# Four-stage residual kernel: expert layers 1 and 2 with both activation parts in one product of 512 columns

## The reference

```python
x = x + L0(x, mask, cond_256, ...)   # attention, 16 heads of 16, RMS norm, modulation
x = x + L1(x, cond_256, ...)         # mixture of 8 experts, the 2 best per token
x = x + L2(x, cond_256, cond_64, ...)# low-rank map, its matrix orthogonalised first
x = x + L3(x, cond_256, ...)         # quaternion rotation
```

```python
h1 = relu(einsum('bsh,ehm->bsem', x, W1) + b1)     # 256 -> 512
h2 = relu(einsum('bsem,emn->bsen', h1, W2) + b2)   # 512 -> 512
out_e = einsum('bsen,enh->bseh', h2, W3) + b3      # 512 -> 256
return einsum('bseh,bse->bsh', out_e, cw)          # cw: softmax weights of the two best experts, else 0
```

## Time and profile before

| | |
|---|---|
| median of 3 runs | 1185.68 us (1181.59 to 1188.18) |
| span of the profiled execution, first to last instruction | 1176.1 us |
| what the page gives of that execution beyond its span | nothing; the median lies 9.6 us above the span |
| TensorE (PE) busy | 1132.8 us, 96% of the span |
| VectorE (DVE) busy | 814.5 us, 69% |
| ScalarE (ACT) busy | 734.6 us, 62% |
| GpSimd (POOL) busy | 524.7 us, 45% |
| expert stage, first to last hidden product | about 628 to 1130 us |

### The profile page before, as it was taken

How to read it: one execution, slowest core, us unless ns; L and a number is a source line. 1 busy time by engine, 2 the same in 40 slices (tenths; PEclk the granted TensorE clock), 3 DMA queues, 4 the chain that set the end, 5 groups by cost and what they waited for, 6 DMA issues and landing times.

```text
span 1176.1 us, 23436 instructions
## 1 busy us (share of the span) xinstructions
PE 1132.8 (96%) x7525; PEld 770.1 (65%) x7582; DVE 814.5 (69%) x2327; ACT 734.6 (62%) x1628; POOL 524.7 (45%) x837
## 2 busy tenths in 40 slices
PE   8899999999999999998988999999999999999988
PEld 4333433434334343342426999999999999999968
DVE  5888888787897878978774444346555555677747
ACT  2466667666676766666566656756666565666645
POOL 8324145583764846747471565346223222222220
PEclk8999999999999999999999999999999999999999
DMA  8655637468275572662726596936665765723536
GB/s 219 205 179 185 211 108 227 132 199 247 86 232 187 171 233 87 219 207 97 279 102 223 160 309 217 360 72 175 175 189 157 224 209 153 248 47 67 164 90 215
DMA packets 101616, 213.65 MB, mean 182 GB/s; under 512 B 10917, under 2 KB 71341, under 8 KB 93046
## 3 DMA queue, kind: packets, MB, share of 16 engines
q1 hardware_dynamic: 86038, 192.42, 49.8%
q0 software_dynamic: 14304, 18.69, 8.7%
q10 hardware_dynamic: 1152, 1.05, 0.4%
HBM read 239.28 MB, written 74.29 MB: 267 GB/s over the span
## 4 chain that ended last, share of the span: by engine, by line
PE 43%; POOL 2%; DMA 2%; DVE 2%; issue 1%; ACT 1%; SPq 1%; POOLq 0%; ACTq 0%
PE bank L1080 37%; PE bank L1239 1%; PE bank L1095 1%; DMA x<-yout,rows 1%; PE bank L1109 1%; PE bank L1199 1%; POOL routed L1952 1%; PE bank L1181 1%; DMA routed<-xw,idx 1%; PE bank L1274 0%; PE bank L1219 0%; POOL run L840 0%; DMA w_parts<-in_W 0%; POOL gt L840 0%; DVE tb L840 0%
## 5 line engine op out<-in xcount | busy, mean ns | idle before, releaser
L1615 DVE CUSTOM_DVE_ANT_0 junk<-bank,mneg 128x512 bf16<-128x512 f32 x512 | 335.6, 683 | 92.1 <-PE bank L1151 91.3
L1347 ACT ACTIVATE pt<-bank 128x512 f32<-128x512 f32 x512 | 301.8, 595 | 150.1 <-PE bank L1166 102.7
L1962 POOL DMA_INDIRECT x<-yout,rows x78 | 123.2, 1579 | 287.3 <-ACT yout L1425 242.7
L1080 PE MATMUL bank<-hid,w 128*128 128x256 f32 x1872 | 243.5, 287 | 3.8 <-DVE hid L1763 3.8
L1080 PEld LDWEIGHTS bank<-hid,w 128*128 128x128 f32 x1872 | 230.1, 191 | 5.7 <-issue 4.3
L1763 DVE TENSOR_TENSOR hid<-full,hid 128x256 fp32r<-128x256 f32 x312 | 132.3, 427 | 142.3 <-ACT full L1420 140.9
L1415 ACT ACTIVATE hid<-bank,biases 128x256 fp32r<-128x256 f32 x312 | 149.3, 479 | 96.1 <-PE bank L1080 94.7
L1166 PE MATMUL bank<-mneg,identb 128*128 128x512 bf16 x391 | 148.7, 380 | 0.0
L1420 ACT ACTIVATE full<-bank,biases 128x256 f32<-128x256 f32 x312 | 148.4, 476 | 0.0
L1080 PE MATMUL bank<-rowsT,w 128*128 128x256 f32 x936 | 123.0, 285 | 1.2 <-issue 1.2
L1181 PE MATMUL bank<-pt,vaug 128*17 128x512 f32 x1024 | 123.2, 599 | 0.7
(11 more groups left out here) (183 smaller groups left out, 1463.8 us busy)
## 6 DMA issues: line engine op xcount, KB each, us to landing
w<-split_weights SPq DMA_DIRECT2D x80, 1024.0 KB
w<-split_weights SPq DMA_DIRECT2D x40, 2048.0 KB
split_weights<-w_parts SPq DMA_DIRECT2D x64, 512.0 KB, 3.8
w_parts<-in_W SPq DMA_DIRECT2D x64, 256.0 KB, 4.5
split_parts<-parts SPq DMA_DIRECT2D x28, 384.0 KB, 2.6
rows<-routed SPq DMA_DIRECT2D x39, 258.0 KB, 3.6
stacks<-split_parts SPq DMA_DIRECT2D x36, 256.0 KB, 5.2
qst<-split_parts SPq DMA_DIRECT2D x24, 256.0 KB, 5.0
```

Of the source, the lines that this page charges most:

```text
L1080: product = T.matmul(ps, w[p], x[q], start=(k == 0 and n == 0), stop=(k == len(weights) - 1 and n == 2))
L1347: A.activation(pt[n % len(pt)][:, :], bank[3 + n % 2][:, :], ACT.Exp, scale=float(D) ** -0.5).then_inc(exped.sem, 1)
L1615: V.tensor_tensor_reduce(junk[n % 2][:, :], bank[n % 3][:, :], mneg[:, 0, st, :], 1.0, FLOOR, ALU.add, ALU.max, rowmax[gi % 2][:, hh, st:s ...
L1962: G.indirect_dma_start(x2_dram, bass.IndirectOffsetOnAxis(ap=rows[j % NS][:, tt, E + 1:E + 2].bitcast(U32), axis=0), yout[j % NY][:, tt], ...
```

## The change

Layers 1 and 2 keep the high and low part of an activation next to each other in one buffer, 256 + 256 columns. `wide_products` multiplies the high weight by both in one product of 512 columns, into all 512 columns of the bank, and the low weight by the high part in one of 256 columns, into the left half. So a block takes two products in place of three, and the sum of the two halves of the bank is the result. Layer 3 keeps its three products; only its indices change.

The halves are added outside TensorE. For each hidden step ScalarE now reads the right half with the bias (Identity) into `full`; VectorE adds the left half to it (`hidden_sum`, which also frees the bank); ScalarE takes ReLU of that, rounded, as the high part (`rectified`); VectorE computes max(full, 0) minus the high part (`hidden_low`). The second instruction of each engine is put behind the first one of the next hidden step: `rectify_hidden` and `split_hidden` run after the next step's first instruction, at the start of `layer3`, and at the start of `layer2(0, 0)`. At the end TensorE issues 16 more products of 512 columns, behind the last one of the program: 12 over 48 rows, in turn on the lower and the upper half of the array's rows, and 4 over all rows. Nothing reads them.

```diff
--- before.py
+++ after.py
@@ -577,8 +577,7 @@
 
 
     def tile_buffers(i):
-        return ([sb(f"rowsT{i}_{n}", [P, KT, TW], F32R) for n in range(2)], [sb(f"hid1_{i}_{n}", [P, HT, TW], F32R) for n in range(2)],
-                [sb(f"hid2_{i}_{n}", [P, HT, TW], F32R) for n in range(2)])
+        return (sb(f"rowsT{i}", [P, KT, 2, TW], F32R), sb(f"hid1_{i}", [P, HT, 2, TW], F32R), sb(f"hid2_{i}", [P, HT, 2, TW], F32R))
...
     rows_high = signal("rows_high", of("turn"))
-    rectified = signal("rectified", [(n, *at) for s, *at in order for n in (1, 2) if s == f"layer{n}"])
+    hidden_at = [(n, *at) for s, *at in order for n in (1, 2) if s == f"layer{n}"]
+    hidden_rest = signal("hidden_rest", hidden_at)
+    rectified = signal("rectified", hidden_at)
...
-    hidden_low = signal("hidden_low", [(n, *at) for s, *at in order for n in (1, 2) if s == f"layer{n}"])
+    hidden_sum = signal("hidden_sum", hidden_at)
+    hidden_low = signal("hidden_low", hidden_at)
...
-        freed = summed.at(tuple(at)) if name == "last" else rectified.at((int(name[-1]), *at))
+        freed = summed.at(tuple(at)) if name == "last" else hidden_sum.at((int(name[-1]), *at))
...
                     product = T.matmul(ps, w[p], x[q], start=(k == 0 and n == 0), stop=(k == len(weights) - 1 and n == 2))
+            return product
+
+        def wide_products(ps, weights, factors):
+            for k, ((high_part, low_part), x) in enumerate(zip(weights, factors)):
+                last = k == len(weights) - 1
+                both = x.rearrange("p n t -> p (n t)")
+                if last:
+                    T.matmul(ps[:, 0:TW], low_part, x[:, 0], start=False, stop=False)
+                product = T.matmul(ps[:, :], high_part, both, start=(k == 0), stop=last)
+                if not last:
+                    T.matmul(ps[:, 0:TW], low_part, x[:, 0], start=False, stop=False)
             return product
...
-                products(ps[:, 0:TW], [weights_of(j, 0, k * M + m * P, k * M + (m + 1) * P) for k in range(KT)],
-                         [[x[:, k, :] for x in rowsT[j % 2]] for k in range(KT)]).then_inc(multiplied[0].sem, 1)
+                wide_products(ps, [weights_of(j, 0, k * M + m * P, k * M + (m + 1) * P) for k in range(KT)],
+                              [rowsT[j % 2][:, k] for k in range(KT)]).then_inc(multiplied[0].sem, 1)
...
                 pe.wait_ge(*hidden_low.at((1, j, HT - 1)))
-                products(ps[:, 0:TW], [weights_of(j, 1, k * M + m * P, k * M + (m + 1) * P) for k in range(HT)],
-                         [[x[:, k, :] for x in hid1[j % 2]] for k in range(HT)]).then_inc(multiplied[1].sem, 1)
+                wide_products(ps, [weights_of(j, 1, k * M + m * P, k * M + (m + 1) * P) for k in range(HT)],
+                              [hid1[j % 2][:, k] for k in range(HT)]).then_inc(multiplied[1].sem, 1)
...
-                products(ps[:, 0:E], [[x[:, k, tt * P:(tt + 1) * P] for x in hid2[j % 2]] for k in range(HT)],
+                products(ps[:, 0:E], [[hid2[j % 2][:, k, n, tt * P:(tt + 1) * P] for n in range(2)] for k in range(HT)],
...
                          [[a[b % 2][:, k * E:(k + 1) * E] for a in (ab_hi, ab_lo)] for k in range(KT)]).then_inc(finished.sem, 1)
             else:
                 side_stage(step)
+        pe.wait_ge(*finished.at((B - 1, ST - 1)))
+        for n in range(6):
+            for half in range(2):
+                lanes = x2T_hi[0][half * 64:half * 64 + 48, 0]
+                T.matmul(bank[4 + half][:, :], lanes[:, n % 4 * P:(n % 4 + 1) * P], lanes, start=True, stop=True)
+        for n in range(4):
+            T.matmul(bank[4 + n % 2][:, :], x2T_hi[0][:, 0, n * P:(n + 1) * P], x2T_hi[0][:, 0], start=True, stop=True)
...
+
+        unrectified = []
+
+        def rectify_hidden():
+
+            for n, j, m in unrectified:
+                if j >= 2:
+                    act.wait_ge(*last_product(n, j - 2))
+                act.wait_ge(*hidden_sum.at((n, j, m)))
+                A.activation((hid1, hid2)[n - 1][j % 2][:, m, 0], full[(hidden_sum.value[n, j, m] - 1) % len(full)][:, :],
+                             ACT.Relu).then_inc(rectified.sem, 1)
+            unrectified.clear()
...
-                A.activation(rowsT[j % 2][0][:, :, :].rearrange("p k t -> p (k t)"), ps[:, :], ACT.Copy).then_inc(rows_high.sem, 1)
+                A.activation(rowsT[j % 2][:, :, 0], ps[:, :].rearrange("p (k t) -> p k t", k=KT), ACT.Copy).then_inc(rows_high.sem, 1)
             elif name in ("layer1", "layer2"):
                 n = int(name[-1])
                 j, m = at
                 ps, _ = hidden_bank(step)
+                place = hidden_sum.value[n, j, m] - 1
+                column = (n - 1) * HT + m
+                if step == ("layer2", 0, 0):
+                    rectify_hidden()
                 act.wait_ge(*multiplied[n - 1].at((j, m)))
                 act.wait_ge(*biases_loaded(j))
-                if j >= 2:
-                    act.wait_ge(*last_product(n, j - 2))
-                column = (n - 1) * HT + m
-                A.activation((hid1, hid2)[n - 1][j % 2][0][:, m, :], ps[:, 0:TW], ACT.Relu,
-                             bias=biases[j % NS][:, column:column + 1])
-                place = rectified.value[n, j, m] - 1
                 if place >= len(full):
                     act.wait_ge(hidden_low.sem, place - len(full) + 1)
-                A.activation(full[place % len(full)][:, :], ps[:, 0:TW], ACT.Relu,
-                             bias=biases[j % NS][:, column:column + 1]).then_inc(rectified.sem, 1)
+                A.activation(full[place % len(full)][:, :], ps[:, TW:2 * TW], ACT.Identity,
+                             bias=biases[j % NS][:, column:column + 1]).then_inc(hidden_rest.sem, 1)
+                rectify_hidden()
+                unrectified.append((n, j, m))
             elif name == "layer3":
                 j, tt = at
+                rectify_hidden()
                 act.wait_ge(*y_biased.at((j, tt)))
                 A.activation(yout[j % NY][:, tt], yout[j % NY][:, tt], ACT.Copy,
...
+
+        unsplit = []
+
+        def split_hidden():
+
+            for n, j, m in unsplit:
+                hi, lo = ((hid1, hid2)[n - 1][j % 2][:, m, part] for part in range(2))
+                if j >= 2:
+                    dve.wait_ge(*last_product(n, j - 2))
+                dve.wait_ge(*rectified.at((n, j, m)))
+                V.scalar_tensor_tensor(lo, full[(hidden_sum.value[n, j, m] - 1) % len(full)][:, :], 0.0, hi.bitcast(F32),
+                                       ALU.max, ALU.subtract).then_inc(hidden_low.sem, 1)
+            unsplit.clear()
...
@@ -1749,20 +1795,23 @@
             elif name == "turn":
                 j, = at
                 ps, _ = misc_bank(step)
-                hi, lo = (rowsT[j % 2][n][:, :, :].rearrange("p k t -> p (k t)") for n in range(2))
+                hi, lo = (rowsT[j % 2][:, :, n] for n in range(2))
                 dve.wait_ge(*rows_high.at((j,)))
-                V.tensor_tensor(lo, ps[:, :], hi.bitcast(F32), ALU.subtract).then_inc(rows_split.sem, 1)
+                V.tensor_tensor(lo, ps[:, :].rearrange("p (k t) -> p k t", k=KT), hi.bitcast(F32), ALU.subtract).then_inc(rows_split.sem, 1)
             elif name in ("layer1", "layer2"):
                 n = int(name[-1])
                 j, m = at
-                hi, lo = (part[:, m, :] for part in (hid1, hid2)[n - 1][j % 2])
-                h = full[(rectified.value[n, j, m] - 1) % len(full)]
-                if j >= 2:
-                    dve.wait_ge(*last_product(n, j - 2))
-                dve.wait_ge(*rectified.at((n, j, m)))
-                V.tensor_tensor(lo, h[:, :], hi.bitcast(F32), ALU.subtract).then_inc(hidden_low.sem, 1)
+                ps, _ = hidden_bank(step)
+                place = hidden_sum.value[n, j, m] - 1
+                if step == ("layer2", 0, 0):
+                    split_hidden()
+                dve.wait_ge(*hidden_rest.at((n, j, m)))
+                V.tensor_tensor(full[place % len(full)][:, :], ps[:, 0:TW], full[place % len(full)][:, :], ALU.add).then_inc(hidden_sum.sem, 1)
+                split_hidden()
+                unsplit.append((n, j, m))
             elif name == "layer3":
                 j, tt = at
+                split_hidden()
                 dve.wait_ge(*multiplied[2].at((j, tt)))
```

## The result

The changed kernel takes 1194.39 us (median of 5 runs, 1193.78 to 1195.04) against 1185.68 us for the kernel before on the same chip: ratio 1.0076, 95% interval 1.0057 to 1.0095. It is slower, where 1172.4 us was forecast and 1161 to 1185 given as the range. On a second chip the ratio was 1.0106 (1.0087 to 1.0125).

A forecast was written before the change was run, and what follows sets the result against it. The prediction took the expert stage as bound by TensorE's product price, set by the weight load. Terms -19.2 + 2.5 + 1.4 + 1.0 + 0.6 + 0.4 = -13.3 us gave 1172.4 us, range 1161 to 1185.

The forecast's parts named there:

- The bound: Expert stage: bound by the price of a TensorE product in a row of them, 119.4 ns.
- the first term: Products of layers 1 and 2: 20.5 ns saved per block, 936 blocks, -19.2 us.
- the two bounds of the step: Wide product in layers 1 and 2: 218 ns as taken, or 239 ns if fp32r is priced by column, gaining nothing.
- own sign of being wrong: In the timeline: wide products starting 0.24 us apart; also PE waiting at layer 2 in every tile.
- the column sets the price: Rival for layers 1 and 2: products give 0 to 2.5 us, 5.9 us of waits stay, 1189 to 1191.5 us; chance 0.11.
- Tile 0: Start of layer2(0, 0): last layer 1 subtraction stands behind attention's last transpose on VectorE; +1.4 us (0 to 2).
- Routing steps: PE waits at 793.69 and near 700 us: ReLU and bank release now hang on VectorE too; +1.0 us (0 to 4).
- The building of the last matrices: Tiles beside it: VectorE side steps make the last subtraction about 0.8 us late in two tiles; +2.5 us (0 to 6).
- The elimination stretch: Tiles beside elimination steps: low parts ready with margins of 0.6 us, so no wait of PE on VectorE.
- The last tile: No layer 1 covers it; chain grows by an addition and a hop beyond the 1.48 us wait: +0.6 us.
- The 16 products: End of the program: they end at 1175.5 to 1176.8 against the span's 1176.1; +0.4 us (0 to 0.7).
- The rival of a late split in every tile: Subtraction of layer1 m = 3 about 1 us late in each of 38 tiles: about 1210 us; chance 0.10.

The follow-up runs named there:

- three_products: Changed kernel, but high weights multiply high and low part in two products of 256 columns instead of one of 512: 1194.82 us, ratio 1.0119 to the kernel before.
- flush_first: Changed kernel, but ReLU and subtraction of layer1(0, 3) issued at once instead of at layer2(0, 0): 1187.50 us, ratio 1.0075 to the kernel before.
- dve_load: Kernel before plus one VectorE addition of 256 columns behind every subtraction from tile 1 on, on its own buffer: 1189.08 us, ratio 1.0052.
- no_defer: Changed kernel with each ReLU and subtraction issued right behind its own first half, not the next step's: 1293.70 us, ratio 1.0922 to the kernel before.
- trains: Kernel before plus trains of 16 products each (fp32r 512 to 8 columns, bf16 512 and 256) behind its last product; fp32r 512 started 0.232, then 0.227 us apart.
- base_again: Kernel before, unchanged, run once more for a second profile: single execution 1177.85 us, span 1176.1 us.

## Why the prediction was wrong

**The bound** was read rightly: TensorE's products set the pace of the tiles; all the time lost is in places where another engine takes over.

**The step that failed** is the first term, "Per block 3 x 119.4 = 358.2 ns becomes 218.3 + 119.4 = 337.7 ns": -19.2 us forecast, -5.7 us measured. It rested on taking the price of 512 columns from a bf16 row and on ascribing the 8 ns between a bare load and 119 ns to a handover. The runs showed 0.233 us for the wide product in the kernel (0.227 to 0.232 in a train) and 6.0 ns saved per block (three_products), and products of 192 columns and fewer start every 0.11 us, so the 119 ns were no load with a handover. The measured price lies between the two bounds of the step, 218 and 239 ns, and nearer to the upper one. The prediction's own sign of being wrong, wide products 0.24 us apart, came almost to the number. Its rival, "the column sets the price", had 0.11 and gave 1189 to 1191.5 us; that it comes near the 1194.39 measured is in part luck, since it had 2.5 us or less of gain and 5.9 us of waits where there were 5.7 and some 17. The rule that I weighed there from the Trainium skill, "TensorE: Matmul & The Clock Gate", section "Back-to-back issue gap", N / 2.4 + 2.5 ns, fits bf16 (0.215 and 0.108 us measured) and not fp32r. By it the term is 2.5 ns by 936, so -2.3 us and not -2.5.

**Tile 0** had place and mechanism right. It was sized at +1.4 us and measured 3.2 (flush_first): the half clock behind the idle stretch, 1.7 us by the estimate above, was left out.

**Routing steps** were named with +1.0 us and an upper end of 4. Measured: 1.4 + 1.6 + 4.5 = 7.5 us in three stretches of the table, some 3 of it through half clock. The step "+1.0 us for both" failed in not following the chain through the blocked queue: it passes there twice. How much of the rest is that and how much is load stays open (dve_load).

**The building of the last matrices** had +2.5 us (0 to 6); 4.9 measured, 3.9 of it shown as VectorE's load. I counted lateness in one slot of two tiles, and the queue was full over five tiles.

**The elimination stretch** was right: the schedule worked gave no wait, and from 820 us on there is none. **The last tile** (+0.6) had its wait as forecast (2.03 us for 1.48). The stretch to the first `turn_x2` grew by 1.0 us, and by 2.3 in the first profile, with its half clock; dve_load has +1.6 there without a longer wait, so the load has a part in it. **The 16 products** (0 to 0.7) cost nothing that can be told. **The rival of a late split in every tile** did not happen; no_defer shows what it would be without the deferral, 100 us.

The sum by measured terms is -5.7 + 3.2 + 7.5 + 4.9 + 1.0 = +10.9 us, against +11.2 between the transposes of tile 0 and the end in the table (9.1 of the spans and 2.1 that attention was quicker). That they agree so well is partly luck: -5.7 counts all 39 tiles, while the other terms from the table already hold the gain of their own tiles. With the first term as forecast, the same waits would have left 2.6 us of gain. That is an upper estimate: the waits were not measured with cheaper products, and where VectorE sets the time cheaper products give nothing (33 to 38, three_products).

## What to carry to other kernels

Take the price of a product from a row of its own type and width; a row of another type is a bound, not a value, and when two limits lie within 10% of each other, a short train of products tells them apart. Where a chain between engines is lengthened, follow each new hop through the queue that is blocked longest, and count the half clock that may follow: here the two longest new waits of TensorE each brought 3.4 us or more of it. A gain of TensorE that is paid in VectorE's time belongs only in the stretches where VectorE has room: confined to those, the same edit gave 0.9954; applied everywhere, it gave 1.0076.

## What the runs showed of the hardware

At the full clock fp32r products of 256 and 512 columns start 0.12 and 0.227 us apart at the end of a train, bf16 ones 0.108 and 0.215. At half clock that difference is gone. The second train of 512 columns fell into such a stretch (windows and timeline of trains):

```profile
1189.70:1193.00 3.30, 3.30 (x9) 2.58 (x8) 0.00 (x0) 0.00 (x0) 0.00 (x0) 0.50 0.00 0
```

```profile
1190.20 2.77 PE L1290 MATMUL bank<-w 128*128 128x512 f32 x6
...
1191.91 1.06 PE L1290 MATMUL bank<-w 128*128 128x512 f32 x2
```

The second line is the fifth product from the first, so they start (1191.91 - 1190.20) / 4 = 0.427 us apart. bf16 products of 512 columns in a half-clock stretch of attention do the same, (563.90 - 562.20) / 4 = 0.425 us (timeline of base_again):

```profile
562.20 0.63 PE L1162 MATMUL bank<-qst,kst 98*128 98x512 bf16 x1
...
563.90 0.63 PE L1166 MATMUL bank<-mneg,identb 128*128 128x512 bf16 x1
```

What costs fp32r the difference at the full clock is open. The clock fell in the train without a hole in TensorE's queue, behind 64 products of 192 to 8 columns that started every 0.11 us.
